# One block for feed-forward, attention and output, and a gate through PSUM, in a two-layer kernel

## The chip, the cores and the metric

The kernel runs on one core of a Trainium2 chip. The core has five engines with a program each: PE (TensorE, matrix products), DVE (VectorE), ACT (ScalarE), POOL (GpSimd) and SP (SyncE, which here only starts DMAs). They meet through semaphores. SBUF has 128 partitions; PSUM has 8 banks of 512 float32 per partition. The metric is the device time of one launch in microseconds (us).

## The reference, cut to what matters

All data are float32. The input x has 2 sequences of 1024 tokens with 512 features. Each layer computes `x = x + s * silu(ffn(layernorm(x)))`, with s its attention.

```python
# layer 0: attention across the heads of one token, and a mixture of experts (2 of 3)
scores = einsum('bsdh,bseh->bsde', q, k) / 4;  s = einsum('bsde,bseh->bsdh', softmax(scores), v)
gate_scores = softmax(concat([h, ratio]) @ gate_w + gate_b)   # 3 experts, ratio of mean |h| of two spans
top_val, top_idx = top_k(gate_scores, 2);  top_val /= sum(top_val) + 1e-8
moe = sum_i top_val[..., i] * expert[top_idx[:, 0, i]](h)     # tanh, gelu or silu between two products
# layer 1: causal attention (32 heads of 16, 8 heads of keys, rotary), 4-bit feed-forward
s = softmax(causal(q @ k.T / 4)) @ v;  out = s_joined @ Wo.T
ffn = (silu(x @ Wg) * (x @ Wu)) @ Wd      # 1376 inner features; x = x + out * silu(ffn)
```

## The kernel before

A product of two float32 matrices is made of three matmuls on high and low parts (function `three`, L37 to L39, where those matmuls are recorded whatever calls it): ACT or DVE rounds a value to its high part, and DVE subtracts to get the low part.

The program has five blocks, one after the other. Each ends with all engines meeting, and a block's own tiles (prefix `c_`, `d_`, `f_`, `g_` for the four of layer 1) are allocated when it begins, so that its loads start then.

- **layer0** (L42). Four chunks of 512 tokens. Each takes 8 steps m: PE makes first products, ACT the expert function, DVE splits its result (L574 to L583), PE makes the second product. Between those, DVE and POOL do the attention across heads, one token tile at a time: POOL multiplies (`pa` L222, `pb` L231, 128x2048 each), DVE sums (`sc` L519, `so` L534). At step m = 3 DVE makes the chunk's `gate`: some 14 small instructions (128x4) on `gexp` and `gt` in SBUF, from which the coefficients `coef` come. In chunk 0 it also makes the ratio of the second sequence: `weigh(1)` (L443) at m = 4, `route(1)` (L462) at m = 6. After the last product of the last chunk, `finish` multiplies and adds per tile, with ACT's silu of each tile in the same PSUM bank 0 (`gate_ready`, `x1_ready`).
- **layer1_projections**. Queries and keys go to scratch in HBM, values stay in `v_all`.
- **layer1_ffn** (L1150). Six steps over the 1376 inner features (five of 256, a last one of 96), each as a loop over two pairs of token quarters: `gate_up` (24 matmuls per quarter and tile), ACT's silu, DVE's product and split (L1289, L1291), `down` (12 matmuls into banks 4 to 7), and `gather`, DVE's addition of four banks to `acc` (L1301). In the last step no weights of a next one are unpacked, so a step there is one quarter after the other. The gate's and the up product's banks are 0 and 1 for the first quarter of a pair, 2 and 3 for the second.
- **layer1_attention** (L1485). 16 groups of four heads. Before a group's scores can be made in the form used here (the row maximum is part of the product), 48 first maxima are needed: an item is one matmul of queries and keys into a spare bank (L1733) and one DVE maximum (L1674, or L1677 where no mask falls). The items of a group are done beside the group before, but those of group 0 stand alone at the start. Then the maxima are turned (L1740), written as rows by DMA, and 24 half units follow: scores (L1751) to two pairs of banks, ACT's exp (L1654), POOL's mask, weighed values (L1769), and twice a turn and a division (L1778, L1696).
- **layer1_output** (L1816). `Wo` is turned (L1933) and split. Then, in a loop over 16 tiles: POOL joins heads (`ct`), PE turns (L1941), ACT and DVE split, PE makes the projection (12 matmuls), DVE multiplies with the gate acc * (1 + tanh) and adds x, and SP writes the tile.

Order is fixed by hand: each engine runs its function in the order of the text. The item's bank and the use that frees it are found by its number, `number % 3` over the banks 0, 1 and 7.

Of the kernel before, what the change touches and what calls it, by code (L numbers as in the profile page):

```python
# [41 lines left out]
def layer0(nc, x, Wq, bq, Wk, bk, Wv, bv, gate_w, gate_b, w1, b1, w2, b2, ident_d, strength_d, x1_d):  # L42

    with ExitStack() as ctx:
# [45 lines left out]
        gt = sb("gt", [P, 6, TPC])  # L90
        coef, coef2 = sb("coef", [P, TPC, SL]), sb("coef2", [P, TPC, SL])
# [3 lines left out]
        rsum = bank[:, 1, D:3 * D].rearrange("p (u d) -> p u d", u=2)  # L95
        b2f = t0[0:BR, 0]
# [39 lines left out]
        def project_bank(t):  # L136
            return bank[:, (0, 2, 3, 0)[t]]

# [122 lines left out]
        def _(act):  # L261
# [66 lines left out]
            def gate_silu(c, t):  # L328
# [4 lines left out]
                if t >= 1:  # L333
                    act.wait_ge(x1_ready, c * TPC + t)
                act.activation(bank[:, 0], moe[:, t], ACT.Silu).then_inc(gate_ready, 1)
# [71 lines left out]
        def _(dve):  # L407
# [131 lines left out]
            def gate_shift(c):  # L539
                lg = qkv[:, :, QB:QB + EXPERTS]  # L540
                dve.tensor_reduce(gt[:, 0], lg, AX.X, ALU.max)
                dve.drain()
                dve.tensor_tensor(gl[:, :, :], lg, gt[:, 0].rearrange("p (t o) -> p t o", o=1).broadcast_to([P, TPC, EXPERTS]),
                                  ALU.subtract).then_inc(gl_ready, 1)

            def gate(c):
                b = c // 2
                dve.wait_ge(gexp_ready, c + 1)
                dve.tensor_reduce(gt[:, 0], gexp[:, :, :], AX.X, ALU.add)
                dve.tensor_tensor(gt[:, 1], gexp[:, :, 0], gexp[:, :, 1], ALU.max)  # L550
                dve.tensor_tensor(gt[:, 2], gexp[:, :, 0], gexp[:, :, 1], ALU.min)
                dve.drain()
                dve.tensor_tensor(gt[:, 3], gt[:, 1], gexp[:, :, 2], ALU.min)
                dve.tensor_tensor(gt[:, 4], gt[:, 1], gexp[:, :, 2], ALU.max)
                dve.drain()
                dve.tensor_tensor(gt[:, 5], gt[:, 3], gt[:, 2], ALU.max)
                dve.scalar_tensor_tensor(out=gt[:, 0], in0=gt[:, 0], scalar=1e-8, in1=gt[:, 4], op0=ALU.mult, op1=ALU.add)
                dve.drain()
                dve.tensor_tensor(gt[:, 0], gt[:, 0], gt[:, 5], ALU.add)
                dve.drain()  # L560
                dve.reciprocal(gt[:, 1], gt[:, 0])
                dve.drain()
                dve.tensor_tensor(gt[:, 4], gt[:, 4], gt[:, 1], ALU.mult)
                dve.tensor_tensor(gt[:, 5], gt[:, 5], gt[:, 1], ALU.mult)
                dve.drain()
                for i, dst in enumerate((coef, coef2)):
# [75 lines left out]
            for c in range(CHUNKS):  # L642
# [7 lines left out]
                for m in range(NF):  # L650
# [16 lines left out]
                    if m == 3:  # L667
                        gate(c)
# [5 lines left out]
                    if c == 0 and m == 4:  # L674
                        weigh(1)
# [1366 lines left out]
```

## Time and profile before

| | us |
|---|---|
| median of 3 runs (lowest, highest) | 1578.92 (1576.87, 1580.47) |
| the profiled execution, and its span | 1579.7, 1578.0 |
| PE busy, of the span | 1368.8 (87%) |
| DVE busy | 1082.8 (69%) |
| ACT busy | 617.5 (39%) |
| POOL busy | 334.0 (21%) |

The mean granted clock of TensorE is 0.927. The five blocks end near 355, 503, 949, 1504 and 1578 us. The page's lists are read as follows: a row of a group gives its number of instructions, busy time, the mean of one, and the idle time of the engine just before them with what ended it; a timeline gives start and length of each run of equal instructions.

### The profile page before, as it was taken

What the parts mean: (1) busy time and instruction counts of PE and PEld (TensorE: products, weight loads), DVE (VectorE), ACT (ScalarE), POOL (GpSimd) and SP (SyncE); (2) the same over time, 40 slices, a digit from 0 to 9 for tenths busy, and PEclk for the clock granted to TensorE, in tenths of its full rate; (3) what the DMA queues carried; (4) which work ended last, traced back from release to release, by engine and by line L of the source; (5) the groups of instructions that cost most, each with busy time, mean ns of one, the idle gap of its engine ahead of it and who ended that gap; (6) DMA issues with size and microseconds to landing.
All of it is one profiled execution on the core that took longest, in us unless ns stands there. A gap on an engine that the chain in (4) does not pass through costs nothing. (4 is left out here: it accounts for less than half of the span.)

```text
span 1578.0 us, 21144 instructions
## 1 busy us (share of the span) xinstructions
PE 1368.8 (87%) x6642; PEld 937.2 (59%) x6642; DVE 1082.8 (69%) x2491; ACT 617.5 (39%) x859; POOL 334.0 (21%) x387
## 2 busy tenths in 40 slices
PE   3778898954885499999999986999999999999968
PEld 3556675743663377777777753555555555555447
DVE  6787978784563555555554437888888888888247
ACT  3643654533331011111111110466666566666622
POOL 2654565622221000000000000122221222122211
PEclk9989999987898699999999985799999999999979
DMA  6002200005443100000100004021112211220042
GB/s 227 30 1 80 81 0 27 27 0 179 157 156 132 51 20 21 20 21 20 30 12 15 5 0 99 2 59 34 32 32 49 44 32 31 42 52 2 2 155 86
DMA packets 47104, 81.48 MB, mean 52 GB/s; under 512 B 8676, under 2 KB 16180, under 8 KB 47012
## 3 DMA queue, kind: packets, MB, share of 16 engines
q1 hardware_dynamic: 45022, 78.67, 17.2%
q10 hardware_dynamic: 1990, 1.68, 0.3%
q8 instruction: 46, 0.75, 0.2%
q14 instruction: 46, 0.38, 0.1%
HBM read 55.80 MB, written 24.26 MB: 51 GB/s over the span
## 5 line engine op out<-in xcount | busy, mean ns | idle before, releaser
L1654 ACT ACTIVATE f_prob<-f_bank 128x1024 f32<-128x1024 f32 (+3 forms) x384 | 301.9, 810 | 187.6 <-PE f_bank L1751 183.6
L1674 DVE CUSTOM_DVE_ANT_0 f_bank<-f_bank,f_mask 128x128 f32<-128x128 f32 (+3 forms) x512 | 247.6, 504 | 67.6 <-PE f_bank L1733 54.6
L1733 PE MATMUL f_bank<-f_kst,f_qst 96*128 96x512 f32 (+3 forms) x768 | 270.9, 398 | 14.7 <-DMA f_qst<-q_scr 12.5
L1733 PEld LDWEIGHTS f_bank<-f_kst,f_qst 96*128 96x128 f32 x768 | 148.2, 197 | 161.7 <-DVE f_mx L1674 58.4
L1751 PE MATMUL f_bank<-f_qst,f_kst 98*128 98x512 f32 (+3 forms) x768 | 210.1, 357 | 1.2 <-ACT f_prob L1654 1.2
L1622 POOL TENSOR_SCALAR_AFFINE_SELECT f_prob<-f_prob 128x256 f32<-128x256 f32 x256 | 103.9, 406 | 434.5 <-ACT f_prob L1654 431.0
L1677 DVE TENSOR_REDUCE f_mx_first<-f_bank 128x1 f32<-128x512 f32 x256 | 175.8, 687 | 5.8 <-PE f_bank L1733 4.2
L1769 PE MATMUL f_bank<-f_prob,f_vst 128*32 128x512 f32 (+3 forms) x1536 | 164.5, 500 | 1.0 <-ACT f_prob L1654 0.9
L1339 ACT ACTIVATE d_hs<-d_bank 128x512 f32<-128x512 f32 (+1 forms) x44 | 26.3, 598 | 348.1 <-PE d_bank L39 348.1
L37 PE MATMUL d_bank<-xtl,d_wgh 128*128 (+1 forms) x352 | 143.2, 407 | 8.8 <-DMA d_zz<-z_gu_scr 8.8
L1751 PEld LDWEIGHTS f_bank<-f_qst,f_kst 98*128 98x128 f32 x768 | 130.2, 192 | 19.7 <-ACT f_prob L1654 9.3
L39 PE MATMUL d_bank<-xth,d_wgh 128*128 (+1 forms) x352 | 140.3, 399 | 0.0
L38 PE MATMUL d_bank<-xth,d_wgl 128*128 (+1 forms) x352 | 139.7, 397 | 0.0
L1289 DVE TENSOR_TENSOR d_hs<-d_hs,d_bank 128x512 f32<-128x512 f32 (+1 forms) x44 | 30.2, 687 | 133.4 <-ACT d_hs L1339 133.4
L1611 POOL COPY f_vst<-v_all 128x256 f32<-128x256 f32 x16 | 6.3, 397 | 458.4 <-POOLq L1152 458.4
L37 PE MATMUL bank<-xtl,w1h 128*128 128x512 f32 x128 | 58.0, 453 | 41.8 <-DVE al L583 39.2
L231 POOL TENSOR_TENSOR pb<-at,qkv 128x2048 f32<-128x2048 f32 x16 | 73.5, 4597 | 80.2 <-DVE so L534 60.4
L37 PEld LDWEIGHTS d_bank<-xtl,d_wgh 128*128 128x128 f32 (+1 forms) x352 | 65.8, 187 | 34.9 <-issue 19.1
L222 POOL TENSOR_TENSOR pa<-qkv 128x2048 f32<-128x2048 f32 x16 | 73.0, 4564 | 46.4 <-DVE qkv L515 26.5
L37 PE MATMUL d_bank<-d_wdl,d_hh 128*128 128x512 f32 (+1 forms) x176 | 71.9, 409 | 9.1 <-DVE acc L1301 7.8
L39 PEld LDWEIGHTS d_bank<-xth,d_wgh 128*128 128x128 f32 (+1 forms) x352 | 65.8, 187 | 17.0
L38 PEld LDWEIGHTS d_bank<-xth,d_wgl 128*128 128x128 f32 (+1 forms) x352 | 65.8, 187 | 15.9
(254 smaller groups left out, 2453.7 us busy)
## 6 DMA issues: line engine op xcount, KB each, us to landing
f_qst<-q_scr SPq DMA_DIRECT2D x32, 384.0 KB, 6.3
wst<-L_ffn_w SPq DMA_DIRECT2D x8, 1024.0 KB, 6.6
q_scr<-c_qh SPq DMA_DIRECT2D x32, 256.0 KB
f_kst<-k_scr SPq DMA_DIRECT2D x32, 192.0 KB, 5.3
d_qw<-L_ffn_qweight_gu SPq DMA_DIRECT2D x40, 128.0 KB, 2.6
xb<-L_attn_x SPq DMA_DIRECT2D x4, 1024.0 KB, 6.8
x_d<-xb SPq DMA_DIRECT2D x4, 1024.0 KB, 4.3
c_xb<-x_d SPq DMA_DIRECT2D x4, 1024.0 KB, 7.8
```

Source lines behind the costliest of these rows:

```text
L37: pe.matmul(out, wh, ml, start=first, stop=False)
L38: pe.matmul(out, wl, mh, start=False, stop=False)
L39: return pe.matmul(out, wh, mh, start=False, stop=last)
L222: pool.tensor_tensor(pa[:, :, :, :], q, k, ALU.mult).then_inc(p1_done, 1)
L231: pool.tensor_tensor(pb[:, :, :, :], a, v, ALU.mult).then_inc(p2_done, 1)
L1622: pool.affine_select(out=p, in_=p, compare_op=ALU.is_ge, fill=0.0, base=0, pattern=[[0, 2], [1, P]], channel_multiplier=-1).then_inc(maske ...
L1654: act.activation(prob[:, c // 2 % 2, c % 2 * 2:c % 2 * 2 + 2, lo:], score_bank[c % 2][:, :, lo:], ACT.Exp, scale=D ** -0.5).then_inc(exp_d ...
L1674: dve.tensor_tensor_reduce(sc, sc, mask[:, CH - w:CH], 1.0, LEAST, ALU.add, ALU.max, mx[:, u, h % 2, h // 2, q:q + 1]).then_inc(spare_free, 1)
L1677: dve.tensor_reduce(mx_first[:, h % 2, h // 2, q:q + 1], sc, AX.X, ALU.max).then_inc(spare_free, 1)
L1733: pe.matmul(spare[v][:, 0:w], qst[0:M_ROW, u, h // 2, q * P:q * P + P], kst[0:M_ROW, u, h % 2, at:at + w], start=True, stop=True).then_inc ...
L1751: mm = pe.matmul(score_bank[c % 2][:, hh, lo:], kst[0:M_ROW + 2, u, hh, k * P:k * P + P], qst[0:M_ROW + 2, u, c % 2, h * CH + lo:(h + 1) * ...
L1769: mm = pe.matmul(sum_bank[2 * D * hh:2 * D * (hh + 1), lo:], vst[:, u, k], prob[:, i % 2, hh, lo:], start=(k == 0), stop=(k == last))
```

## The change

In layer 0 the intermediates of the gate move to PSUM bank 1 (`gp`, `coef2`) and a small SBUF tile (`gs`), such that no instruction of it reads two operands from SBUF; one copy and one drain are added per gate. The gate moves from step 3 to step 4, `weigh(1)` from 4 to 3, `route(1)` from 6 to 5, and the start of DVE's program is put in another order. The last chunk's silus use the banks 0, 2, 3, 0 in turn.

The three blocks `layer1_ffn`, `layer1_attention` and `layer1_output` become one, `layer1_rest`, whose tiles have fixed addresses (`place`, in KB). ACT's queue loads the constants at the block's start. The last feed-forward step is written out: 32 of group 0's 48 items stand between its matmuls, in pairs, and use the banks 0 and 1 alone; its quarters after the first all use the banks 2 and 3. `ctx_sb` lies where the high part of x was, the residual rows where its low part was, `Wo` in part of `v_all`; they are loaded in the groups 8 to 11. `Wo` is turned in the last group, and so are the first two tiles of the context; the output's loop is written out.

```diff
@@ layer0, DVE
             def gate(c):
+                first, higher, middle, top, second = (gp[:, i] for i in range(5))
+                total, lower, inverse = (gs[:, i] for i in range(3))
                 dve.wait_ge(gexp_ready, c + 1)
-                dve.tensor_reduce(gt[:, 0], gexp[:, :, :], AX.X, ALU.add)
-                dve.tensor_tensor(gt[:, 1], gexp[:, :, 0], gexp[:, :, 1], ALU.max)
-                dve.tensor_tensor(gt[:, 2], gexp[:, :, 0], gexp[:, :, 1], ALU.min)
+                dve.tensor_reduce(total, gexp[:, :, :], AX.X, ALU.add)
+                dve.tensor_copy(first, gexp[:, :, 0])
+                dve.drain()
+                dve.tensor_tensor(higher, first, gexp[:, :, 1], ALU.max)
+                dve.tensor_tensor(lower, first, gexp[:, :, 1], ALU.min)
...
-            second_biases()
-            masks(0)
+            statistics(2)
             dve.wait_ge(row_ps, 1)
...
-            statistics(2)
             projected(0, 0)
+            second_biases()
             projected(0, 1)
             low_part_w1(0)
-            token_logits(1)
             projected(0, 2)
+            masks(0)
             projected(0, 3)
+            token_logits(1)
...
-                    if m == 3:
+                    if m == 4:
                         gate(c)
-                    if c == 0 and m == 4:
+                    if c == 0 and m == 3:
                         weigh(1)
+                    if c == 0 and m == 5:
+                        route(1)
                     if c == 0 and m == 6:
-                        route(1)
                         masks(1)
@@ layer1_rest
+        def gate_slot(s, b, u, n):
+            return slot(s, u, n) if s < LAST else 0 if isinstance(b, int) and b * 2 + u == 0 else 1
...
+        def spare_bank(number):
+            return spare[number % 2 if number < NI else number % SPARE]
...
+        def freed(number):
+            return number - 1 if number < NI else number if number < NI + SPARE else number - SPARE + 1
@@ DVE
+            dve.wait_ge(const_in, 48)
+            clear(0)
+            product(LAST, 0, 0, 0)
+            clear(1)
+            clear(2)
+            for q in range(1, CHUNKS):
+                first = (q - 1) * 12 - 8
+                for i in range(4 if q > 1 else 0):
+                    items(first + 2 * i)
+                product(LAST, q // 2, q % 2, 0, lambda: items(first + 8))
+                gather(LAST, (q - 1) // 2, (q - 1) % 2, range(0, 2))
+                items(first + 10)
+                gather(LAST, (q - 1) // 2, (q - 1) % 2, range(2, 4))
+            items(BESIDE - 4)
+            gather(LAST, 1, 1, range(0, 2))
+            items(BESIDE - 2)
+            gather(LAST, 1, 1, range(2, 4))
+            for s in range(BESIDE, NI):
+                item(0, s, s)
+            maxima(0, NI)
@@ PE
+            gate_up(LAST, 0, 0, 0)
+            for q in range(1, CHUNKS):
+                first = (q - 1) * 12 - 8
+                if q == 1:
+                    gate_up(LAST, 0, 1, 0)
+                else:
+                    gate_up(LAST, q // 2, q % 2, 0, beside=lambda i: items(first + 2 * i))
+                down(LAST, (q - 1) // 2, (q - 1) % 2, 0, beside=lambda i: items(first + 8 + 2 * i))
+            down(LAST, 1, 1, 0, beside=lambda i: items(BESIDE - 4 + 2 * i))
+            for s in range(BESIDE, NI):
+                item(0, s, s)
...
+                    if n == NG - 1 and c in WO_STEPS:
+                        turn_weights(WO_STEPS.index(c))
+            turn_context(0)
+            turn_context(1)
+            weighed(NG - 1, NU - 1)
+            project(0)
+            turn(NG - 1, 1, TAIL)
+            for t in range(1, TILES):
+                if t + 1 < TILES:
+                    turn_context(t + 1)
+                project(t)
```

`items(first)` does the items `first` and `first + 1`; PE's `beside(i)` is called after every six matmuls. In the function `item` itself nothing is changed but the bank and the use of it that is waited for. `WO_STEPS` are the half units 12, 14, 16 and 18.

DVE's order in layer 0, chunk 0, where the gate stood (`sc` sums the scores, `gexp` holds the exponentials of the gate). Before:

```order
L519 TENSOR_REDUCE sc<-pa 128x256
L521 TENSOR_REDUCE bank<-sc 128x16
L523 TENSOR_TENSOR sc<-sc,bank 128x256
L549 TENSOR_REDUCE gt<-gexp 128x4
L550 TENSOR_TENSOR gt<-gexp 128x4
L551 TENSOR_TENSOR gt<-gexp 128x4
```

And now (`abs_sum` and `weighed` belong to `weigh(1)`):

```order
L527 TENSOR_REDUCE sc<-pa 128x256
L529 TENSOR_REDUCE bank<-sc 128x16
L531 TENSOR_TENSOR sc<-sc,bank 128x256
L451 TENSOR_TENSOR abs_sum<-abs_sum,rstd 128x8
L454 TENSOR_TENSOR weighed<-strength,abs_sum 128x8 x2
...
L560 TENSOR_REDUCE gs<-gexp 128x4
L561 COPY bank<-gexp 128x4
L563 TENSOR_TENSOR bank<-bank,gexp 128x4
L564 TENSOR_TENSOR gs<-bank,gexp 128x4
```

`weigh(1)` stands where the gate began. The gate comes one step later, behind the sums of `so` and the reciprocals, and the operands of its maxima and minima are one in `bank` and one in SBUF.

PE's order at the end of the feed-forward (`d_wdl`, `d_hh` and their like are operands of `down`; `f_kst`, `f_qst` keys and queries). Before:

```order
L38 MATMUL d_bank<-d_wdh,d_hl 128x512
L39 MATMUL d_bank<-d_wdh,d_hh 128x512
L1197 REGISTER_ALU
L1197 COMPARE_AND_BRANCH
L1152 UNCONDITIONAL_BRANCH
L1722 UNCONDITIONAL_BRANCH
L1733 MATMUL f_bank<-f_kst,f_qst 128x128
L1733 MATMUL f_bank<-f_kst,f_qst 128x256
L1733 MATMUL f_bank<-f_kst,f_qst 128x384
L1733 MATMUL f_bank<-f_kst,f_qst 128x512 x2
```

And now, from the first quarter's `down` on (L1812 is the item's matmul, `xtl_2856,wgh_4182` are operands of `gate_up`):

```order
L38 MATMUL d_bank<-wdh_4184,hl 128x512
L39 MATMUL d_bank<-wdh_4184,hh 128x512
L1812 MATMUL d_bank<-kst_4202,qst_4199 128x128
L1812 MATMUL d_bank<-kst_4202,qst_4199 128x256
...
L39 MATMUL d_bank<-wdh_4184,hh 128x512
L1812 MATMUL d_bank<-kst_4202,qst_4199 128x384
L1812 MATMUL d_bank<-kst_4202,qst_4199 128x512
L37 MATMUL d_bank<-xtl_2856,wgh_4182 96x512
...
L39 MATMUL d_bank<-xth_2855,wgh_4182 96x512
L1812 MATMUL d_bank<-kst_4202,qst_4199 128x512
L1812 MATMUL d_bank<-kst_4202,qst_4199 128x128
```

The branches between the blocks are gone, and the items stand in pairs after each six matmuls, from the first `down` on.

PE's order from attention's end to the first projection (L1769 weighed values, L1778 a turn of the context, L1933 a turn of `Wo`, L1941 of a token tile's context, L37 the first matmul of a projection). Before:

```order
L1769 MATMUL f_bank<-f_prob,f_vst 32x512 x4
L1751 MATMUL f_bank<-f_qst,f_kst 128x512 x4
L1769 MATMUL f_bank<-f_prob,f_vst 32x512 x8
L1778 MATMUL f_bank<-f_ident,f_ctxt 128x128 x4
L1490 UNCONDITIONAL_BRANCH
L1925 UNCONDITIONAL_BRANCH
L1933 MATMUL g_bank<-g_ident,g_wn 128x128 x16
L1941 MATMUL g_bank<-g_ident,g_ct 128x128 x4
...
L37 MATMUL g_bank<-g_wol,g_cth 128x512
```

And now (L1836 scores, L1852 weighed values, L1870 a turn of `Wo`, L1880 of a tile's context):

```order
L1836 MATMUL d_bank<-qst_4199,kst_4202 128x384 x2
L1870 MATMUL d_bank<-ident,v_all 128x128 x4
L1836 MATMUL d_bank<-qst_4199,kst_4202 128x384 x2
...
L1836 MATMUL d_bank<-qst_4199,kst_4202 128x512 x2
L1870 MATMUL d_bank<-ident,v_all 128x128 x4
L1836 MATMUL d_bank<-qst_4199,kst_4202 128x512 x2
...
L1836 MATMUL d_bank<-qst_4199,kst_4202 128x512 x4
L1852 MATMUL d_bank<-prob,vst 32x512 x4
L1880 MATMUL d_bank<-ident,ct 128x128 x8
L1852 MATMUL d_bank<-prob,vst 32x512 x4
L37 MATMUL d_bank<-wol,cth 128x512
```

`Wo` is turned between the last group's scores, and the two tiles of the context are turned ahead of the last weighed values; the first projection follows those at once, ahead of the last group's own turn.

## Rows read from the trace of the kernel before

**Rows 1.** Busy time by stretch: us, PE, PEld, DVE, ACT, POOL, clock, DMA, GB/s.

```profile
903.00:993.40 90.40, 67.18 (x205) 43.45 (x204) 49.83 (x126) 4.90 (x8) 0.40 (x1) 0.70 0.22 43
...
1502.80:1521.30 18.50, 6.04 (x26) 4.62 (x25) 4.14 (x7) 3.81 (x7) 2.39 (x4) 0.56 0.78 287
1521.30:1578.00 56.70, 52.52 (x248) 42.88 (x248) 42.92 (x63) 16.45 (x30) 7.38 (x12) 0.95 0.20 74
```

**Rows 2.** Groups of DVE instructions, 48 to 360 us: count | busy us, mean ns | idle.

```profile
L551 DVE TENSOR_TENSOR gt<-gexp 128x4 f32<-128x4 f32 x4 | 9.4, 2346 | 0.0
L550 DVE TENSOR_TENSOR gt<-gexp 128x4 f32<-128x4 f32 x4 | 8.9, 2231 | 0.0
...
L549 DVE TENSOR_REDUCE gt<-gexp 128x4 f32<-128x12 f32 x4 | 0.6, 158 | 0.0
```

**Rows 3.** Timeline of DVE, layer 0: start, us, what, [idle before <- releaser].

```profile
42.80 2.29 DVE L428 TENSOR_TENSOR w1l<-wst,w1h 128x2048 fp32r<-128x2048 f32 x1 [3.48 <-ACT w1h L316]
...
53.54 3.53 DVE L543 TENSOR_TENSOR gl<-qkv,gt 128x12 f32<-128x12 f32 x1
...
86.04 1.29 DVE L550 TENSOR_TENSOR gt<-gexp 128x4 f32<-128x4 f32 x1
87.25 4.57 DVE L551 TENSOR_TENSOR gt<-gexp 128x4 f32<-128x4 f32 x1
...
99.11 3.73 DVE L443 TENSOR_TENSOR abs_sum<-abs_sum,rstd 128x8 f32<-128x8 f32 x1
...
114.83 2.88 DVE L462 TENSOR_TENSOR ratio<-ratio,means 128x1 f32<-128x1 f32 x1
```

**Rows 4.** Timeline of POOL over the same stretch.

```profile
82.65 4.65 POOL L231 TENSOR_TENSOR pb<-at,qkv 128x2048 f32<-128x2048 f32 x1
...
98.29 4.53 POOL L231 TENSOR_TENSOR pb<-at,qkv 128x2048 f32<-128x2048 f32 x1 [6.49 <-DVE so L534]
113.22 4.47 POOL L231 TENSOR_TENSOR pb<-at,qkv 128x2048 f32<-128x2048 f32 x1 [10.41 <-DVE so L534]
```

**Rows 5.** Timeline of ACT at the end of layer 0.

```profile
350.47 0.60 ACT L335 ACTIVATE bank<-moe 128x512 f32<-128x512 f32 x1 [1.59 <-DVE xb L598]
```

**Rows 6.** Timeline of DVE, last feed-forward step to last first maximum.

```profile
914.93 0.68 DVE L1289 TENSOR_TENSOR d_hs<-d_hs,d_bank 96x512 f32<-96x512 f32 x1 [3.40 <-ACT d_hs L1339]
...
940.62 2.47 DVE L1301 TENSOR_TENSOR acc<-acc,d_bank 128x512 f32 x4
...
951.63 3.50 DVE L1662 CAST f_kst<-f_fixed 128x2048 fp32r<-128x2048 f32 x3 [2.08 <-DMA f_fixed<-fixed_d]
...
961.79 0.30 DVE L1674 CUSTOM_DVE_ANT_0 f_bank<-f_bank,f_mask 128x128 f32<-128x128 f32 x1 [6.66 <-issue]
...
987.80 0.14 DVE L1674 DVE_READ_ACCUMULATOR2_ANT f_mx<- 128x1 f32 x1
```

**Rows 7.** Timeline of PE over the same stretch, to the first scores.

```profile
943.22 0.79 PE L37 MATMUL d_bank<-d_wdl,d_hh 96*128 96x512 f32 x1 [3.91 <-DVE acc L1301]
...
961.16 2.50 PE L1733 MATMUL f_bank<-f_kst,f_qst 96*128 96x128 f32 x6 [12.46 <-DMA f_qst<-q_scr]
...
993.39 1.06 PE L1751 MATMUL f_bank<-f_qst,f_kst 98*128 98x512 f32 x2
```

**Rows 8.** Busy time in five of the 48 maxima's 26 us.

```profile
975.00:980.00 5.00, 4.81 (x10) 2.70 (x10) 4.64 (x16) 0.00 (x0) 0.00 (x0) 0.50 0.01 3
```

**Rows 9.** Timeline of PE, end of attention and start of output.

```profile
1500.39 1.07 PE L1769 MATMUL f_bank<-f_prob,f_vst 128*32 128x512 f32 x8 [0.63 <-ACT f_prob L1654]
...
1521.26 0.79 PE L37 MATMUL g_bank<-g_wol,g_cth 128*128 128x512 f32 x1 [3.94 <-DVE g_ctl L1909]
```

**Rows 10.** Chain that ended last, from attention's end on: start, us, what.

```profile
1504.96 15.25 DMA g_x<-x_d
...
1522.47 0.43 PE g_bank L39
...
1526.93 0.23 PE g_bank L38
```

More of the change, by code:

```diff
@@ L1234, in _ @@
                 body(-1, b)
[L1235 removed]
+            for s in range(LAST):
                 scales(s + 1)
@@ L1349, in _ @@
+            low_part(0)
+            low_part(1)
+            normalize(NG - 1, 1, TAIL)
+            dve.wait_ge(x_in, 16 * CHUNKS)
+            for t in range(TILES):
+                finish(t)
+                if t + 2 < TILES:
+                    low_part(t + 2)
         @block.tensor
@@ L1729, in item @@
+                down(s, b, 1, 0)
+                down(s, b, 1, 1)
+            each_pair(pe, body)
+            def item(n, s, number):
+                u, turns = n % STACKS, n // STACKS
                 h, q, at, w = ITEMS[s]
@@ L1779, in turn @@
                 mm.then_inc(spare_ps, 1)
-            def step(c, g, todo, before, after, second):
-                scores(g, c)
-                def run(part):
-                    for number, v, task, s in part:
-                        if task == "items":
-                            item(after, s, number, v)
-                        elif task == "early":
-                            item(second, s, number, v)
-                        elif task == "turn maxima":
-                            maxima(after, number, v)
-                        elif task == "turn half":
-                            turn(g, 0, number, v)
-                        else:
-                            turn(before, 1, number, v)
-                run(todo[:1])
-                if c > 1 and c % 2 == 1:
-                    weighed(g, c // 2 - 1)
-                elif c == 1 and before is not None:
-                    weighed(before, NU - 1)
-                run(todo[1:])
@@ new lines, in _ @@
+            for n in range(NG):
+                for c in range(NC):
+                    scores(n, c)
+                    part = list(todo(n, c))
+                    run(n, c, part[:1])
+                    if c > 1 and c % 2 == 1:
+                        weighed(n, c // 2 - 1)
+                    elif c == 1 and n > 0:
+                        weighed(n - 1, NU - 1)
+                    run(n, c, part[1:])
+                    if n == NG - 1 and c in WO_STEPS:
+                        turn_weights(WO_STEPS.index(c))
```

958 lines of the change are left out of this document (459 added, 499 removed).

## The prediction

> **What bounds the kernel now.** I read busy time by stretch first, since each block has another limit. Two stretches are poor: 903 to 993.4 us, where the feed-forward ends and attention starts (PE 67 of 90 us at a mean clock of 0.70), and 1502.8 to 1521.3, where PE works 6 of 18.5 us while the DMA share is 0.78 [rows 1]. Then the groups of DVE in layer 0, for instructions far above their size. The small instructions of the gate (128x4) should all take what `L549` takes, 0.16 us; `L550` and `L551` take 2.2 and 2.3, 18.3 us in eight instructions [rows 2]. The timelines say why: `L551` starts at 87.25 and ends at 91.8, exactly with POOL's multiplication, which starts at 87.23 (82.65 + 4.65 is the one before it, with which `L550` ends) [rows 3, 4]. The three others of this kind are `L543`, `L443` (its 3.73 us end at 102.8, as does POOL's `pb`, 98.29 + 4.53) and `L462`, under the `pb` that starts at 113.22 [rows 3, 4]. DVE's split is what PE waits for in that block, so such a stall goes to the end. For the later blocks I followed PE and DVE until a block's first needed result: 48 first maxima stand alone from 961.79 to 987.94, and the first scores come at 993.39 [rows 6, 7]; the output's first projection comes at 1521.26, after a load of the residual rows that took 15.25 us [rows 9, 10].
>
> **Layer 0, the gate in PSUM.** An operand in `bank` leaves one in SBUF, so that no instruction of the gate needs the access that POOL holds. The rows show only the stalled case: `L549`, which has one SBUF operand, takes 0.16 us in the mean of all four chunks, just ahead of stalled ones [rows 2]. Taken at 0.16 each, the eight save 18.3 - 8 x 0.16 = 17.0, and `L543`, whose maximum moves to PSUM too, 3.53 - 0.16 = 3.4 [rows 3]. The Trainium skill (SBUF — State Buffer, section Who interferes with whom) says this in general: a DVE instruction with two SBUF inputs contends with a GpSimd instruction that reads SBUF, one with a single SBUF input doesn't; by that rule, the trace agrees, with 4.57 us against 0.16. The same section speaks against one edit, the added copy (first rival).
> The extra copy and its drain have no row; an instruction of 0.16 and a drain of like size give 0.25 a gate, 1.0 for four (bounds 0.6 and 4 x 4.6, fully stalled).
> Moves: `route(1)` at step 5 falls where POOL is idle, between 102.8 and 113.22 [rows 4]: 2.88 - 0.16 = 2.7 saved. `weigh(1)` leaves its place under `pb` (3.73 - 0.16 = 3.6 saved), but now begins where `L550` began, at 86.04 in the trace, and is written as before: its two kinds of product with two SBUF operands would wait for the rest of `pb` and the whole next `pa`, as the two gate instructions do now, 1.29 + 4.57 - 2 x 0.16 = 5.6 lost [rows 3].
> Start: DVE waits 3.48 us for ACT's `w1h` at 39.3 and then splits it [rows 3]. The biases and masks that now stand ahead of it move behind later work; half of that wait is taken as gained, 1.7 (bounds 0 and 3.5).
> Tail: ACT waits 1.59 us for `xb` between two silus of 0.60 because all use one bank, 2.19 per tile [rows 5]; with several banks DVE's two instructions (0.69 each and a drain, 1.4 to 1.5) set the pace, three tiles gain 2.3 (bounds 0 and 3).
> Sum: 17.0 + 3.4 + 3.6 + 2.7 - 5.6 - 1.0 + 1.7 + 2.3 = 24.1. Bounds: 3 if the gate's stalls stay and part of the rest is hidden by PE, 32 if `weigh(1)` meets an idle POOL.
>
> **From the feed-forward to attention.** What the trace shows: PE waits 3.91 us for the last addition and then runs at half clock [rows 7], keys are cleared for 3.50 us at 951.63, PE waits 12.46 us for the load, 26.15 us of items follow, and 5.5 us later come the scores [rows 6, 7]. New: loads need only the cleared buffers. `clear(0)` is now ahead of the first product, near 904; even the full 12.5 us of today's wait end at 917, when the first `down` asks for them.
> Then DVE is the bound. Its product of the second quarter stays where it is, near 915, since PE's `gate_up` ahead of it gets no items. From 915.0 on DVE has the products and splits of three quarters (0.68 + 0.69 each, 4.1), 16 additions (four take 2.47: 9.9) and 48 items (26.1): 40.1 us, so 955.1 with no gap. PE's part in the same time is smaller: 144 matmuls of 0.23 (33.3 us) and 48 items, most of them done while DVE is at the ones before. Pauses I estimate at 5.5: 1.8 before the last `down`, which needs all four additions of the quarter before, as PE's 3.91 today; and 3.7 in the 16 items that stand alone, since with two banks, not three, an item's matmul (up to 0.43 at half clock [rows 10], and the handovers) lies bare for 0.2 each. Last item 960.9, first scores 5.5 later: 966.4 in place of 993.39, a gain of 27.0.
> Bounds: 36.5, with no pause and the turn of the maxima under other work; 12, if the items cost their matmuls and a handover each between `down` matmuls (32 x 0.5) on top. Queued behind DVE's waits for items are the additions, and PE's next `down` waits for these: a late pair delays both engines, which is why I don't take the lower pauses.
> ACT's work there doesn't grow. Its queue issues three constant loads first, when it is idle.
>
> **From attention to the output.** The last weighed values begin at 1500.39 and end at 1501.5 [rows 9]. The residual rows (15.25 us) and `Wo` are loaded in the groups 8 to 11, under attention, and have landed long before. The two first tiles are turned while ACT does the last exps; ACT's high part and DVE's low part (0.6 and 0.69) are done about 1501.8, so the first projection starts about 1502.0: 19.3 earlier than 1521.26. It also finds the clock up: nine of its steps take 0.43 now and 0.23 after a while [rows 10], 1.9 more. Against it: the last group's own turn, now behind the first projection, 0.4; four turns of `Wo` (four matmuls of 128 columns each, an estimated 0.4) and four ACT copies (0.60, as ACT's other copies from a bank [rows 5]) in the last group, where ACT and PE each set the pace at times: 1.5 of these 4.0 taken. Sum 19.3; bounds 15 (all of the 4.0, and the first two divisions late) and 22. The 16 tiles stay at PE's pace of 56.7 us for all [rows 1]; if DVE, which has 42.9 us there, is late with the turned context, that shows in the bounds.
>
> **Sum.** 24.1 + 27.0 + 19.3 = 70.4. The profiled execution took 1579.7, so 1509.3; it stood 0.8 above the median, which gives **1508.5**. With the errors of the three terms taken as independent its own range is 1500 to 1519.
>
> **Rivals.**
> 1. *The gate still stalls* (0.12). The copy SBUF to PSUM, or the reduce, waits for POOL, or the instructions wait although one operand is in PSUM. For it: the gate at step 4 starts soon after POOL takes up a `pb`, and no row shows an instruction with mixed operands under POOL. Against: `L549`. One full multiplication, 4.6 us, less what the gate's new place spares, over four gates is +15: **1523.5**. The section of the skill named above lets `copy` take the shared pair of ports in a fast mode; that would be this rival.
> 2. *The interleaved step runs at half clock* (0.10). Pauses between pairs of items let TensorE fall to 1.2 GHz in the quarters, as it did after 3.9 us of idleness at 943 [rows 7, 10]. Then some 96 matmuls take 0.43 in place of 0.23, +19: **1527**. Against: PE has work during nearly all of it.
> 3. *The clock stays at 2.4 GHz through the items* (0.10). Now it is at 0.50 in the items, though PE is busy 4.81 of 5 us [rows 8]; in the forecast that stays so. If PE arrives without a pause, the lone items' matmuls take 0.39 and the first group starts at full clock: the 3.7 us of bare matmuls go and a little of the first group's start, -4: **1504.5**. The Trainium skill (TensorE: Matmul & The Clock Gate, Part 1: The HAM clock gate) states that sustained activity releases the throttle; rows 8 show high activity at the lower level for five us within a stretch of twenty-six, and here the measurement decides.
> 4. *Slower than before* (0.03). Attention starts at half clock and stays there, since the items' handovers over two banks never let PE's array fill; a group takes 509/16 = 31.8 us today (993.39 to 1502) at full clock, of which PE is busy nearly all, so a group at half clock costs some 27 us more. From the third such group on the gain of 70 is gone, three give **1590**. Against it: today attention leaves the same half clock within its first group.
>
> **How the numbers follow.** Forecast 0.65, the rivals 0.12, 0.10, 0.10, 0.03. The range of 8 in 10 has to hold rivals 1 to 3 and errors of a term: three terms whose bounds lie 10 to 29 apart, so **1492 to 1530**; a lower end of 1492 takes in both upper bounds of the first two terms (8 + 9.5). Faster than before by over 0.2%, about what a measurement of this kernel tells from no change: 0.96; within 0.2%: 0.01; slower: 0.03.
>
> **What the profile after would show.** The gate's instructions at about 0.16 each under POOL's multiplications, one `weigh` product at over 4 us. Layer 0 about 24 us shorter. The first scores 27 us earlier counted from the feed-forward's last weights (near 942 in all); pairs of items between PE's `down` matmuls without DVE waits over 1 us; a half clock at the first scores. The first projection within 1 us of the last weighed values, each tile 3.2 us after the last (56.7 less the ends, by 16). The forecast is wrong if a group of attention takes other than 31.8 us, if DVE waits for PE more than 10 us in the last step, or if a gate instruction still takes over 1 us.

## The result, and the profile after

The changed kernel takes 1521.25 us (median of 4 runs, 1515.89 to 1526.90), the kernel before 1577.89. The ratio is 0.9642 (95% interval 0.9602 to 0.9682), 56.6 us less in the medians. The forecast was 1508.5, its range 1492 to 1530. The profiled execution took 1526.9, the slowest of the four, with a span of 1525.2.

Busy time by stretch in the changed kernel, columns as in [rows 1]. The stretches shown are layer 0, the last feed-forward step up to the first scores, attention, and the output:

```profile
0.00:349.70 349.70, 273.93 (x1066) 207.29 (x1066) 274.37 (x498) 176.22 (x236) 178.84 (x60) 0.90 0.16 53
...
890.20:957.60 67.40, 57.35 (x205) 38.15 (x204) 49.40 (x126) 6.19 (x9) 0.40 (x1) 0.81 0.26 53
957.60:1469.60 512.00, 501.51 (x3178) 284.50 (x3176) 409.06 (x1283) 320.27 (x420) 111.30 (x275) 0.99 0.18 42
1469.60:1525.20 55.60, 51.29 (x256) 41.95 (x252) 43.22 (x65) 18.01 (x32) 7.41 (x12) 1.00 0.20 76
```

The hole between attention and output is gone: the stretch 1502.8 to 1521.3 of [rows 1] has no answer here. The stretch from 903 us, where the last step's first `gate_up` began, to the first scores was 90.4 us at a clock of 0.70. That matmul now starts at 890.19, and from there it is 67.4 us at 0.81, 23.0 less. Layer 0, forecast to end 24 us earlier, ends 5 us earlier in this profile, which is of the slowest run.

DVE's small instructions in layer 0 (count | busy us, mean ns | idle), answering [rows 2, 3]:

```profile
L451 DVE TENSOR_TENSOR abs_sum<-abs_sum,rstd 128x8 f32<-128x8 f32 x1 | 5.8, 5830 | 0.0
L497 DVE TENSOR_SCALAR msk<-msk 128x2 f32<-128x2 f32 x1 | 3.8, 3765 | 0.0
...
L561 DVE COPY bank<-gexp 128x4 f32<-128x4 f32 x4 | 0.8, 196 | 0.0
L563 DVE TENSOR_TENSOR bank<-bank,gexp 128x4 f32<-128x4 f32 x4 | 0.7, 170 | 0.3
...
L564 DVE TENSOR_TENSOR gs<-bank,gexp 128x4 f32<-128x4 f32 x4 | 0.6, 152 | 0.0
```

`L563` and `L564` are the maximum and minimum that took 2.2 and 2.3 us; they take 0.17 and 0.15, the added copy (`L561`) 0.20. `weigh` (`L451`) waits 5.83 us, as forecast. `L497`, the first instruction of `masks(1)`, takes 3.77 us until POOL's `pb` ends; it was not forecast. It is a `tensor_scalar` with one tensor operand, in SBUF: the Trainium skill (SBUF — State Buffer, Who interferes with whom) counts those among the operations that can take the shared ports in a fast mode, when their operands meet conditions. `copy` is in the same list, but the copy to PSUM did not wait: the first of the four stood at 93.08 us, inside a `pb` of 92.23 to 96.76, and the three others (169.16, 244.02, 315.69) also stood inside a multiplication of POOL's.

What PE waited for in layer 0 (us in total, times, longest), in the kernel before:

```profile
PE bank L37 <- DVE al L583: 39.2, 11, 7.5
PE bank L701 <- DVEq L485: 6.5, 1, 6.5
```

and in the changed one:

```profile
PE bank L37 <- DVE al L596: 19.1, 9, 4.7
PE bank L762 <- ACT moe L356: 11.7, 4, 3.8
PE bank L715 <- DVE xtl L430: 8.0, 1, 8.0
PE bank L734 <- DVEq L455: 2.5, 1, 2.5
```

Twenty us of waiting for the split are gone, and 11.7 us of waiting for `moe` are new. Two smaller waits grew with it: PE's turn of the next chunk's tokens (`L701`, now `L715`) waits 8.0 us for DVE, which had 3.77 of stall in `L497` shortly before, and the routing matmul (`L734`) waits 2.5 us for the stalled `weigh(1)`. The four rows of the changed kernel sum to 41.3 us, the two of before to 45.7, so PE waits 4.4 us less in these rows and layer 0 ends 5.2 us earlier. ACT's timeline in chunk 3 of the changed kernel shows where the waits for `moe` come from:

```profile
312.77 0.75 ACT L331 ACTIVATE bank<-bank,b1m,msk 128x512 f32<-128x512 f32 x1
318.64 2.42 ACT L356 ACTIVATE moe<-bank,coef 128x512 f32<-128x512 f32 x4 [5.11 <-DVE coef L583]
```

`L356` is ACT's `first_slot`, which scales the first expert's sums by the coefficients. It waits 5.11 us for the last instruction of the gate (`coef`), and the expert functions of the next step stand behind it. Over the four chunks ACT's wait for `coef` grew too, in the kernel before and in the changed one:

```profile
ACT moe L348 <- DVE coef L570: 7.7, 4, 2.7
```

```profile
ACT moe L356 <- DVE coef L583: 21.3, 4, 8.4
```

The second half of the result, PE from the last `down` to the first scores, and DVE beside it, answering [rows 6, 7]:

```profile
930.99 0.50 PE L37 MATMUL d_bank<-wdl,hh 96*128 96x512 f32 x1 [3.24 <-DVE acc L1596]
...
932.02 0.39 PE L38 MATMUL d_bank<-wdh,hl 96*128 96x512 f32 x1
...
933.63 0.63 PE L38 MATMUL d_bank<-wdh,hl 96*128 96x512 f32 x1
...
957.57 1.05 PE L1836 MATMUL d_bank<-qst,kst 98*128 98x512 f32 x2
```

```profile
902.06 0.68 DVE L1583 TENSOR_TENSOR hs<-hs,d_bank 96x512 f32<-96x512 f32 x1 [1.19 <-ACT hs L1477]
...
933.23 0.69 DVE L1631 TENSOR_REDUCE mx_first<-d_bank 128x1 f32<-128x512 f32 x1 [2.29 <-PE d_bank L1812]
...
936.43 0.69 DVE L1631 TENSOR_REDUCE mx_first<-d_bank 128x1 f32<-128x512 f32 x1 [1.11 <-PE d_bank L1812]
```

PE still waits 3.24 us for the additions ahead of the last `down`. A matmul of 0.39 us up to 932.02 is one of 0.63 at 933.63: the granted clock fell about 1.4 us after PE had resumed. Three windows of the stretch behind it:

```profile
945.00:950.00 5.00, 3.78 (x7) 1.76 (x7) 3.63 (x11) 0.00 (x0) 0.00 (x0) 0.50 0.00 0
...
960.00:965.00 5.00, 5.00 (x18) 2.61 (x17) 3.22 (x11) 2.65 (x3) 1.84 (x5) 0.50 0.01 2
965.00:970.00 5.00, 4.64 (x32) 3.28 (x32) 3.16 (x10) 1.96 (x4) 1.49 (x4) 0.85 0.01 2
```

The clock stays at 0.50 through the maxima that stand alone and comes back at about 966, inside the first group, as before. Between attention and output:

```profile
1468.57 1.07 PE L1852 MATMUL d_bank<-prob,vst 128*32 128x512 f32 x8
1469.61 0.50 PE L37 MATMUL d_bank<-wol,cth 128*128 128x512 f32 x1
...
1472.47 0.60 PE L1860 MATMUL d_bank<-ident,ctxt 128*128 128x128 f32 x4
```

The first projection starts with the last weighed values, at full clock.

### The profile page after: what moved, and what is told of

Its sections match the earlier page's. It is cut to its first block, busy times and chain, and to the rows that moved or that the text cites. A ratio compares the mean times of both kernels' runs of the same rounds, so it can differ in the third digit from the quotient of the medians.

```text
span 1525.2 us, 20789 instructions
## 1 busy us (share of the span) xinstructions
PE 1353.0 (89%) x6642; PEld 930.9 (61%) x6642; DVE 1065.8 (70%) x2495; ACT 618.0 (41%) x859; POOL 334.1 (22%) x387
## 4 chain that ended last, share of the span: by engine, by line
PE 57%; DVE 5%; issue 1%; ACT 1%; DVEq 1%; DMA 0%; SPq 0%; POOL 0%; ACTq 0%; POOLq 0%
PE d_bank L1812 11%; PE d_bank L37 9%; PE d_bank L1852 9%; PE d_bank L1836 8%; PE d_bank L39 8%; PE d_bank L38 8%; DVE d_bank L1628 2%; PE d_bank L1860 1%; DVE mx_first L1631 1%; DVEq L1634 1%; PE d_bank L1738 1%; DVE hl L1586 0%; DVE hs L1583 0%; ACT hh L1485 0%; PE d_bank L1880 0%
## 5 line engine op out<-in xcount | busy, mean ns | idle before, releaser
L1521 ACT ACTIVATE prob<-d_bank 128x1024 f32<-128x1024 f32 (+3 forms) x384 | 303.2, 811 | 220.0 <-PE d_bank L1836 215.6
L1628 DVE CUSTOM_DVE_ANT_0 d_bank<-d_bank,mask 128x128 f32<-128x128 f32 (+3 forms) x512 | 247.4, 503 | 61.2 <-PE d_bank L1812 54.3
L1812 PE MATMUL d_bank<-kst,qst 96*128 96x512 f32 (+3 forms) x768 | 269.2, 391 | 5.9 <-DVE mx_first L1631 2.8
L1812 PEld LDWEIGHTS d_bank<-kst,qst 96*128 96x128 f32 x768 | 146.0, 194 | 153.2 <-DVE mx L1628 56.5
L1836 PE MATMUL d_bank<-qst,kst 98*128 98x512 f32 (+3 forms) x768 | 210.7, 357 | 0.5 <-ACT prob L1521 0.5
L1631 DVE TENSOR_REDUCE mx_first<-d_bank 128x1 f32<-128x512 f32 x256 | 176.3, 689 | 17.1 <-PE d_bank L1812 12.4
L1852 PE MATMUL d_bank<-prob,vst 128*32 128x512 f32 (+3 forms) x1536 | 164.6, 500 | 1.2 <-POOL prob L1447 1.2
L37 PE MATMUL d_bank<-xtl,wgh 128*128 (+1 forms) x352 | 141.7, 402 | 8.9 <-DMA zz<-z_gu_scr 8.9
L1836 PEld LDWEIGHTS d_bank<-qst,kst 98*128 98x128 f32 x768 | 130.3, 192 | 18.8 <-ACT prob L1521 8.2
L38 PE MATMUL d_bank<-xth,wgl 128*128 (+1 forms) x352 | 138.2, 393 | 0.0
L39 PE MATMUL d_bank<-xth,wgh 128*128 (+1 forms) x352 | 138.1, 392 | 0.0
L37 PEld LDWEIGHTS d_bank<-xtl,wgh 128*128 128x128 f32 (+1 forms) x352 | 65.8, 187 | 32.8 <-issue 19.2
L39 PEld LDWEIGHTS d_bank<-xth,wgh 128*128 128x128 f32 (+1 forms) x352 | 65.8, 187 | 15.1
L37 PE MATMUL d_bank<-wdl,hh 128*128 128x512 f32 (+1 forms) x176 | 70.5, 401 | 4.9 <-DVE acc L1596 3.2
L37 PE MATMUL bank<-xtl,w1h 128*128 128x512 f32 x128 | 55.9, 437 | 20.6 <-DVE al L596 19.1
```

The costliest lines, as they stand in the source:

```text
L37: pe.matmul(out, wh, ml, start=first, stop=False)
L38: pe.matmul(out, wl, mh, start=False, stop=False)
L39: return pe.matmul(out, wh, mh, start=False, stop=last)
L1521: act.activation(prob[:, c // 2 % 2, c % 2 * 2:c % 2 * 2 + 2, lo:], score_bank[c % 2][:, :, lo:], ACT.Exp, scale=D ** -0.5).then_inc(exp_d ...
L1628: dve.tensor_tensor_reduce(sc, sc, mask[:, CH - w:CH], 1.0, LEAST, ALU.add, ALU.max, mx[:, u, h % 2, h // 2, q:q + 1]).then_inc(spare_free, 1)
L1631: dve.tensor_reduce(mx_first[:, h % 2, h // 2, q:q + 1], sc, AX.X, ALU.max).then_inc(spare_free, 1)
```

## The experiments

Ten further kernels, each timed beside the kernel before on the same chip. The ratios of nodrain and gate2 have wide intervals, since one of the seven runs of the kernel before beside them took 1587.19 us, so their medians are the better guide. Medians and ratios:

| kernel | median us | ratio (95%) |
|---|---|---|
| changed | 1521.25 | 0.9642 (0.9602 to 0.9682) |
| gate in PSUM, step 3 (ps3) | 1511.99 | 0.9578 (0.9563 to 0.9593) |
| gate in SBUF, step 4 (sb4) | 1542.49 | 0.9774 (0.9760 to 0.9788) |
| gate in SBUF, step 3 (sb3) | 1525.39 | 0.9670 (0.9655 to 0.9684) |
| all 48 maxima alone (alone) | 1534.46 | 0.9730 (0.9713 to 0.9747) |
| before with the changed layer 0 (l0only) | 1568.43 | 0.9942 (0.9927 to 0.9958) |
| Wo's high part by DVE (wodve) | 1522.61 | 0.9661 (0.9646 to 0.9675) |
| three banks for the lone maxima (three) | 1517.28 | 0.9625 (0.9610 to 0.9640) |
| five edits together (best) | 1501.95 | 0.9529 (0.9516 to 0.9542) |
| best, without the added drains (nodrain) | 1500.14 | 0.9492 (0.9456 to 0.9528) |
| best, gate at step 2 (gate2) | 1499.53 | 0.9492 (0.9456 to 0.9528) |

### The gate's memory and its place

```diff
@@ ps3 (and sb3)
-                    if m == 4:
+                    if m == 3:
                         gate(c)
@@ sb4 (and sb3): gate_shift and gate as before
-        gs = sb("gs", [P, 3, TPC])
-        coef = sb("coef", [P, TPC, SL])
+        gt = sb("gt", [P, 6, TPC])
+        coef, coef2 = sb("coef", [P, TPC, SL]), sb("coef2", [P, TPC, SL])
```

ps3: 

> The changed kernel with the gate back at step 3 of each chunk (in PSUM as changed). Theory 1, the place: DVE no longer stalls in the gate, but at step 4 the coefficients come only 1 to 2 us earlier than before; ACT's scaling of the first slot (L356) waits 5.1 us for them, and PE's first matmul of the second slot waits 3.75 us for that, 11.7 us in all, and then runs at half clock. At step 3 that wait goes: layer 0 ends 12 to 20 us earlier (near 332 in place of 349.6), the whole is near 1505. Theory 2, slack: the stall lay beside PE's own work and what PE lost waiting for the split it now loses elsewhere; layer 0 ends within 3 us of 349.6, the whole within 4 us of 1521.

sb4: 

> The changed kernel with the gate's intermediates back in SBUF, at step 4. Theory 1: the stall of 1 to 9 us per gate now comes straight on the late coefficients, ACT and PE wait as much longer: layer 0 longer by 8 to 20 us, the whole 1529 to 1541. Theory 2: no more than 4 us from 1521.

sb3: 

> The changed kernel with the gate in SBUF and at step 3, both as before (start, tail and the two routing steps as changed). Theory 1: coefficients at the time of before, the gate's two halves of the change cancel: layer 0 within 4 us of 349.6, the whole 1518 to 1526; with the two runs above the table shows that memory and place each cost or bring over 8 us and not their sum. Theory 2: like the changed kernel too, but then the two others also are.

PE's waits in layer 0, in ps3:

```profile
PE bank L37 <- DVE al L596: 22.8, 10, 4.7
```

in sb4 (`L755` is the matmul of the second slot's bias):

```profile
PE bank L755 <- ACT moe L354: 24.7, 4, 6.9
PE bank L37 <- DVE al L589: 19.3, 10, 3.1
```

and in sb3:

```profile
PE bank L37 <- DVE al L589: 36.4, 12, 7.5
```

In ps3 no row names `moe`, and ACT's `first_slot` in chunk 3 has no idle time ahead of it:

```profile
303.03 0.75 ACT L331 ACTIVATE bank<-bank,b1m,msk 128x512 f32<-128x512 f32 x1
303.71 2.41 ACT L356 ACTIVATE moe<-bank,coef 128x512 f32<-128x512 f32 x4
```

ACT's wait for `coef` in sb3 is 8.9 us in all, near the 7.7 of the kernel before, and PE has no wait for `moe` there either.

In ratios, PSUM in place of SBUF brings 0.0092 at step 3 and 0.0132 at step 4 (14.5 and 21 us of 1577); step 4 in place of 3 costs 0.0064 in PSUM and 0.0104 in SBUF (10 and 16 us). The edit did both, which leaves 0.0028, 4.4 us, and with an interval of 0.0040 to either side for the changed kernel that may also be nothing. Theory 1, the place, stands: PE waits for `moe` in both kernels with the gate at step 4 (11.7 us in PSUM, 24.7 in SBUF) and in neither with step 3. Theory 2 falls, since the four kernels lie 30 us apart. For layer 0 of ps3 12 to 20 us less were expected, and in the profiles it ends 15.6 us earlier (334.0), but the whole took 1512 and not near 1505, since only 10 us came in the medians. sb4 took 1.5 us more than the 1541 that bounded its range, and sb3 lay inside its own.

gate2 moves it one step more:

> The kernel with all five edits, the gate at step 2 in place of 3. If the coefficients were still late at step 3 for ACT's first slot: some us less in layer 0. If the place matters only until the coefficients are ahead of that, as the missing wait of PE for moe says: no change beyond 2 us, 1500 to 1504.

It took 1499.53, and nodrain (below), which ran beside it, 1500.14. The two differ by more than the gate's place, though: gate2 keeps the drains that nodrain leaves out. Against best, from which it differs by the place alone, it is 2.4 us lower, but timed on another chip; in profiles its layer 0 ends at 328.1 and that of best at 330.4, while the same layer 0 varies by 7.7 us between profiles (last section). So whether step 2 brings some 2 us or nothing stays open.

### How much of the change is layer 0

l0only is the kernel before with the function `layer0` of the changed one; nothing else is edited.

> The kernel before with layer 0 of the changed one: the three other blocks and their addresses as before. If the parts add up, it is layer 0's share alone: 5 to 10 us faster than before, 1568 to 1573. Two theories on the feed-forward's matmuls, whose mean length is 397 ns (L39) in the one profile of before and 390 in all five profiles with the fixed map: addresses, and it is 397 here again, with some 5 us of feed-forward between the two layouts; or the run, and it may be 390 here.

By its ratio it is 9.1 us faster than before (6.6 to 11.5), within the 5 to 10 expected. The mean duration of the feed-forward's `L39` matmuls from 555 to 860 us (count | busy us, mean ns), in the kernel before, in l0only and in the changed kernel:

```profile
L39 PE MATMUL d_bank<-xth,d_wgh 128*128 x270 | 107.2, 397 | 0.0
```

```profile
L39 PE MATMUL d_bank<-xth,d_wgh 128*128 x269 | 106.8, 397 | 0.0
```

```profile
L39 PE MATMUL d_bank<-xth,wgh 128*128 x271 | 105.6, 390 | 0.0
```

It is 397 ns with the old addresses in both profiles and 390 with the new in each of the ten profiles that have them, at a granted clock of 1.00. From the first sums copied to `acc` (564.15 and 557.58) to the product of the last step's second quarter (914.93 and 902.06) the changed kernel takes 6.3 us less. l0only shows that layer 0 and the run are not the cause. But the ten kernels have both the new addresses and one block in place of three, and no run moved a tile alone: that the addresses do it is likely and not shown.

### The maxima beside the last step

```diff
@@ alone: items() returns at once on DVE and PE
-BESIDE = 32
+BESIDE = 0
```

> The changed kernel with none of group 0's 48 maxima beside the last feed-forward step (all stand alone after it, on two banks). If the interleaving hides them: 32 items at the 0.76 us of the 16 that stand alone now are 24 us, less the 3 us by which the last additions come earlier: first scores 21 us later, the whole near 1542. If interleaving only moves their cost into the quarters (each pair delays PE's products and DVE's additions by its own length): under 8 us later, the whole under 1529.

13 us slower than the changed kernel, between the two. From the product of the second quarter (902.06 here, 890.10 there) to the first scores it takes 67.8 us there and 55.5 here. The last addition ends 24.8 us after that product there, 36.6 here: 32 maxima beside the step cost it 11.8 us, and save the 24 that they cost alone. Half of their cost is hidden.

```diff
@@ three
         def spare_bank(number):
-            return spare[number % 2 if number < NI else number % SPARE]
+            return spare[number % 2 if number < BESIDE else (number + 1) % SPARE if number < NI else number % SPARE]
         def freed(number):
-            return number - 1 if number < NI else number if number < NI + SPARE else number - SPARE + 1
+            return (number - 1 if number < BESIDE + 2 else number - SPARE + 1 if number < NI
+                    else number if number < NI + SPARE else number - SPARE + 1)
@@ PE: acc_ready is waited for ahead of item 34, the first in bank 7
```

> The changed kernel with three banks (0, 1, 7) for the 16 first maxima that stand alone, in place of two. They take 12.1 us now, 0.76 each, against 0.54 in the kernel before (three banks). If the bank handover is the cause: 8.7 to 9.5 us, first scores 2.5 to 3.4 us earlier. If the half clock is: 12 us still.

DVE from the last additions to the merge of the maxima, in the changed kernel and in three:

```profile
937.38 0.14 DVE L1628 DVE_READ_ACCUMULATOR2_ANT mx<- 128x1 f32 x1
...
950.82 0.17 DVE L1636 TENSOR_TENSOR mx<-mx,mx_first 128x16 f32<-128x16 f32 x1
```

```profile
930.90 0.14 DVE L1629 DVE_READ_ACCUMULATOR2_ANT mx<- 128x1 f32 x1
...
941.22 0.17 DVE L1637 TENSOR_TENSOR mx<-mx,mx_first 128x16 f32<-128x16 f32 x1
```

From the end of the additions (938.66 and 932.18) it is 12.2 us with two banks and 9.0 with three, at the same half clock: the handover was the cause. The medians differ by 4.0 us; in the profiles the stretch from the second product to the first scores is 3.1 us shorter (52.4 and 55.5).

### Wo in the last group, and the drains

```diff
@@ wodve: DVE's turn_weights; ACT's is dropped
-                dve.wait_ge(wo_hi, o + 1)
+                dve.wait_ge(wo_tp, o + 1)
+                dve.tensor_copy(woh[:, :, o * P:o * P + P], k4(spare[o % SPARE])).then_inc(wo_hi, 1)
+                dve.drain()
```

> The changed kernel, the high part of Wo copied by DVE and not by ACT in the last group. If ACT's exps set the pace there, so that four copies of 0.60 and their waits are the 2.5 to 4.6 us by which the last group is longer than before: 2 to 3 us faster, last group 32 to 33 us from its first turn. If PE's four turns of Wo are the cost: no change over 0.5 us.

No change: 1522.61, and from the last group's turn of maxima to its last weighed values 34.24 us for 34.43. So ACT's copies were not what lengthened that group (31.95 us in the kernel before), and the reading that they were fell, unless DVE's copies cost as much there. What is left is PE's part: four turns of `Wo` (0.35 to 0.38 each) and two of the context (1.03 together) take 2.5 us, which is the whole difference. No run took them away.

```diff
@@ nodrain: normalize
-                dve.drain().then_inc(ctx_ready, 1)
+                if n == NG - 2 and h == 1:
+                    dve.drain().then_inc(ctx_ready, 2 * HKV)
+                if n == NG - 1:
+                    dve.drain().then_inc(ctx_ready, HKV)
```

> The kernel with all five edits (1502 us), without the drain and the ctx_ready increment that the changed kernel adds to each division of the context (two per group; only the last two groups keep them). Groups 2 to 15 take 32.1 us in all seven profiles of the fixed map and 31.9 in both of the old one. If the added drain on DVE is the cause: 31.9 again, 3 us faster, 1499. If it is something else (addresses, the written-out loop): 32.1 still, 1502.

The turn of the maxima, once per group, in the changed kernel and in nodrain (last figures: first and last start):

```profile
L1825 PE MATMUL d_bank<-ident,mx x16: 269/270/372, 951.1 to 1435.2; 128*32 128x128 f32 x16
```

```profile
L1833 PE MATMUL d_bank<-ident,mx x16: 269/270/372, 926.8 to 1408.6; 128*32 128x128 f32 x16
```

Fifteen groups take 484.1 us and 481.8 (484.3 in best, from which nodrain differs by the drains alone). Without the first, groups are 32.09 us long in the changed kernel and 31.95 in nodrain, and 31.95 in the kernel before: the added drains cost 0.15 us per group, some 2 us in all and not 3. As a whole nodrain is 1.8 us below best, timed on another chip. In its profile the last group also fell to half clock for a part, 1.9 us more than in best; the last group of each, best first:

```profile
1412.00:1446.50 34.50, 31.12 (x218) 14.48 (x218) 7.96 (x15) 24.05 (x32) 8.63 (x20) 1.00 0.01 2
```

```profile
1410.80:1444.80 34.00, 31.70 (x205) 14.48 (x197) 7.59 (x13) 23.13 (x31) 8.63 (x20) 0.90 0.00 1
```

### All together

best has the gate at step 3, `three`, `wodve`, the additions of the third quarter ahead of two maxima, and `weigh` through PSUM:

```diff
@@ weigh
-                dve.tensor_tensor(abs_sum[:, tiles], abs_sum[:, tiles], rstd[:, tiles], ALU.mult)
+                dve.tensor_copy(aw, rstd[:, tiles])
+                dve.drain()
+                dve.tensor_tensor(aw, aw, abs_sum[:, tiles], ALU.mult)
@@ DVE, last step
-                gather(LAST, (q - 1) // 2, (q - 1) % 2, range(0, 2))
+                gather(LAST, (q - 1) // 2, (q - 1) % 2, range(0, 2 if q < CHUNKS - 1 else 4))
                 items(first + 10)
-                gather(LAST, (q - 1) // 2, (q - 1) % 2, range(2, 4))
+                if q < CHUNKS - 1:
+                    gather(LAST, (q - 1) // 2, (q - 1) % 2, range(2, 4))
```

> The changed kernel with all that the runs so far point to: gate at step 3 in PSUM; the weighing of the second sequence through PSUM too (5.83 us of stall should become 0.2, layer 0 some 4 us less, if DVE is what chunk 0 waits for); three banks for the maxima alone (-3); the additions before the last down not behind two maxima (-1.2 of PE's 3.24); Wo's high part on DVE (-2.5). Sum 10.7 on the 1512 of the run with the gate at step 3: 1501. If parts hide behind each other as the gate's did, 1505 to 1510.

It took 1501.95, as expected, 0.9529 of before and 19 us under the changed kernel. That the sum came out is in part luck: of its 10.7 us, 2.5 were for `wodve`, which brought nothing by itself, and 1.2 for the additions, while from the second product to the first scores best takes the 52.4 us of `three` alone. Some 3 of the 10 us that came are in none of these parts, and no run tells where they come from. DVE's instructions there:

```profile
L500 DVE TENSOR_SCALAR msk<-msk 128x2 f32<-128x2 f32 x1 | 3.7, 3722 | 0.0
...
L454 DVE TENSOR_TENSOR bank<-bank,abs_sum 128x8 f32<-128x8 f32 x1 | 0.2, 175 | 0.1
L452 DVE COPY bank<-rstd 128x8 f32<-128x8 f32 x1 | 0.2, 172 | 0.0
```

The weighing (`L452`, `L454`) takes 0.2 each in place of 5.83; `L500`, the `tensor_scalar` of the masks, still waits 3.7. Layer 0 ends at 330.4, 3.6 us before that of ps3 in single profiles:

```profile
0.00:330.40 330.40, 259.85 (x1066) 198.86 (x1066) 268.67 (x500) 176.51 (x236) 179.10 (x60) 0.95 0.16 57
```

## Why the prediction was right, and where it was 13 us off

The direction held, none of the four rivals came, and the last two terms were near. That the time lies well inside the range is in part luck: 7.7 us came that no term named, and without them it would have been about 1529, at the range's upper end. By parts, in the two profiles (before, changed):

| | forecast | measured |
|---|---|---|
| layer 0 | 24.1 | 5.2 in these profiles; 9.1 in l0only's runs |
| projections and feed-forward before the last step | 0 | 7.7 |
| feed-forward to first scores | 27.0 | 22.9 |
| attention and output | 19.3 | 17.0 |
| sum | 70.4 | 52.8 (56.6 in medians) |

**Layer 0: the step that failed is "Moves".** It priced `route(1)` and `weigh(1)` and put at nothing, without a reason, what waits for the gate, which the change also moved, from step 3 to 4. ACT's `first_slot` stands at step 5 of ACT's order and needs the coefficients; PE's second slot needs `first_slot`. In chunk 3 `first_slot` started at 319.96 us before, behind the stalled gate, and at 318.64 now, behind the quick gate a step later. So the stall went and a wait took its place: PE's 39.2 us on `al` became 19.1 on `al` and 11.7 on `moe`. The term for the stalls was 20.4 (17.0 and 3.4); at its old step the memory is worth 14.5 by the runs, so that the term was 6 too large there, and at step 4 21. The missing term is the place, -10. With the two, 24.1 becomes about 8, near the 9.1 of l0only.

**The smaller terms of layer 0.** `weigh(1)` lost 5.8 (forecast 5.6 with both instructions). `route(1)` does run in POOL's gap, but the 2.7 saved were given back by `L497` (3.77), which now meets `pb`: I had looked for instructions with two SBUF operands alone, though the section that the prediction cites for them sets its rule outside the fast modes. The first split `L596` came 2.1 us earlier (52.70 and 50.59; forecast 1.7) and, in the tail, from the first addition of `finish` to the last it is 6.57 us before and 4.11 now, 2.5 (forecast 2.3).

**Feed-forward to scores.** The forecast had 46.0 us from the second product (914.93) to the last maximum (its own terms, 40.1 and 5.5, give 960.6 and not 960.9), and 5.5 to the scores; measured are 48.7 and 6.8. The lone maxima took 12.2, as forecast (8.7 and 3.7 of pauses). Around the last `down` DVE waited 3.4 (2.29 and 1.11), where 1.8 stood; and in the quarters before, where none stood, 3.4 in waits of 0.3 to 0.7 for the pairs' matmuls. Of the 5.0 us more of waiting 2.7 remain at the last maximum (where the rest was made up was not traced), and 1.3 came between it and the scores. The sign "DVE waits of under 1 us between the pairs" was missed with them. Rival 2 did not happen in the quarters (0.39 us per matmul until 932), only in the last `down`; rival 3 neither: at 945 the clock is 0.50 with PE busy 3.78 of 5 us. The statement of the Trainium skill that sustained activity releases the throttle (TensorE: Matmul & The Clock Gate, Part 1: The HAM clock gate) is not tested by that stretch, where PE pauses at every handover. In the first group, with PE busy for 5.00 of 5 us from 960, the clock was still at 0.50, and it came back at about 966. Rival 1 fell with `L563`'s 0.17, rival 4 with groups of 32.1 us. The prediction called it a sign of error if a group took other than 31.8 us; half of those 0.3 us are the drain, and the kernel before has 31.95 by the same count.

**Attention to output.** The gap of 19.8 us between last weighed values (1501.46) and first projection closed wholly, and the 16 tiles took 55.6 for 56.7. Attention took 4.0 more from its first scores to its last weighed values. From the first turn of the maxima it is 5.4 more: 2.0 for the drain in the groups 2 to 15, which I had named in no term, 0.9 in the first group, at half clock for a part (33.7 to 34.8 us in the profiles, whatever the edit), and 2.5 in the last, where 1.5 was taken for the turns of `Wo` with ACT's copies and nothing for the two turns of the context. Of this 5.4, 1.4 falls ahead of the first scores.

**What was not forecast at all** is the 7.7 us before the last step, of which 6.3 come with the shorter matmuls.

## What to carry to other kernels

An instruction that stalls has two costs, the time on its own engine and the time at which its result comes; when it is made quick and moved in one edit, read what waits for its result in every other engine's order before counting the first. A work item interleaved into a busy step is hidden only as far as the step's own engine has gaps: here 32 maxima cost 12 us beside and 24 alone. And in a relay between two engines the number of buffers counts: an item took 0.76 us with two banks and 0.56 with three.

## What the runs showed of the hardware

- The feed-forward's matmul of 512 columns has a mean of 397 ns in the kernels with the old SBUF addresses and three blocks (two profiles) and 390 in those with the new addresses and one block (ten), at the same granted clock.
- The same layer 0 took from 341.9 to 349.6 us in five profiles. Its chunk 1 (130 to 200 us) in the changed kernel and in alone, columns as in [rows 1]:

```profile
130.00:200.00 70.00, 64.09 (x257) 48.45 (x256) 56.66 (x89) 39.42 (x49) 39.94 (x10) 0.90 0.14 46
```

```profile
130.00:200.00 70.00, 64.31 (x280) 50.26 (x279) 57.65 (x92) 39.57 (x49) 44.12 (x10) 0.98 0.14 46
```

The granted clock is 0.90 in one and 0.98 in the other. The last group of attention shows the same (0.90 or 1.00, about 2 us). Such half-clock stretches may explain part of the spread of 11 us among the changed kernel's four runs, but that is not shown: their mean clocks (0.938, 0.941, 0.939 and 0.941 for 1526.90, 1522.69, 1519.81 and 1515.89 us) do not follow their times.
- A `tensor_scalar` of 128x2 with a single SBUF operand waited 3.77 us for POOL's multiplication, and one of 128x4 (`L425` at 54.51) took 1.06 us, until POOL's work of 50.97 to 55.55 ended. One of 128x1 took 0.15 us under such a multiplication (kernel before, `L458` at 114.37), and so did, with 0.20 us, each of the four copies of 128x4 from SBUF to PSUM. So a small size is no protection.
